# Relation sums of a graph network: rows of x3 W gathered from edges sorted on the chip, in place of dense count tables

## The reference

```python
def rgcn(x, src, dst, edge_type, weight, root, bias):
    out = x @ root + bias
    for r in range(8):
        mask = edge_type == r
        sums = segment_sum(x[src] * mask[:, None], dst, num_segments=1250)
        cnt = segment_sum(mask, dst, num_segments=1250)
        out = out + (sums / maximum(cnt, 1)[:, None]) @ weight[r]
    return out

u = rgcn(x3, ...)
z = concatenate([u, x3], axis=1) @ w_gate + b_gate
h = tanh(u) * z + x3 * (1 - z)
out = layernorm(x3 + h)
```

## Time and profile before

| what | us |
|---|---|
| runs of the kernel, median of 3 | 3798.32 |
| lowest and highest of them | 3790.24, 3836.48 |
| span of the profiled execution (first to last instruction) | 3698.9 |
| median less the profiled span | 99.4 |
| PE, DVE, ACT, Pool busy in that span | 3462.3, 2038.9, 939.7, 1363.0 |

### The profile page before, as it was taken

The page is one execution under the profiler, slowest core; times in us unless marked ns, Lnnn a source line. Parts: engine busy times, 40 slices in busy tenths (PEclk is TensorE's granted clock), DMA queues, the critical chain, the costliest instruction groups (busy, mean ns, idle before and its releaser), DMA issues.

```text
span 3698.9 us, 55829 instructions
## 1 busy us (share of the span) xinstructions
PE 3462.3 (94%) x22823; PEld 2642.5 (71%) x22823; DVE 2038.9 (55%) x4393; ACT 939.7 (25%) x1365; POOL 1363.0 (37%) x1094
## 2 busy tenths in 40 slices
PE   5898868999999999989989979899999999999998
PEld 4566556899899899934434478677777777777798
DVE  7877656432433454364443367777676544444477
ACT  0112313111211312222222266342222122222134
POOL 3767625566455567757777211300000000000021
PEclk8999989999999999989999989999999999999999
DMA  8789785543643455544554355543432422222233
GB/s 286 197 258 280 252 288 145 158 123 82 180 120 95 138 179 163 165 146 158 167 165 137 113 220 186 175 178 108 147 128 74 143 78 82 71 82 72 70 109 107
DMA packets 268704, 557.27 MB, mean 151 GB/s; under 512 B 94954, under 2 KB 118143, under 8 KB 266430
## 3 DMA queue, kind: packets, MB, share of 16 engines
q1 hardware_dynamic: 124504, 384.00, 29.6%
q10 hardware_dynamic: 64520, 116.89, 8.9%
q0 software_dynamic: 79424, 52.83, 8.8%
HBM read 370.13 MB, written 183.44 MB: 150 GB/s over the span
## 4 chain that ended last, share of the span: by engine, by line
PE 70%; DVE 11%; DMA 7%; POOL 6%; issue 4%; ACT 2%; SPq 1%; ACTq 0%; POOLq 0%; DVEq 0%
PE ps L442 50%; PE ps L825 11%; DMA EM<-ee,adr 2%; POOL EM L2483 2%; PE ps L447 2%; POOL gl L2493 2%; POOL gr L2493 2%; DVE eqj L989 2%; DVE eqj L986 2%; DMA slab<-T 1%; PE ps L710 1%; PE ps L712 1%; PE ps L711 1%; PE ps L491 1%; PE ps L492 1%
## 5 line engine op out<-in xcount | busy, mean ns | idle before, releaser
L442 PE MATMUL ps<-a,yy 128*128 128x384 f16 (+5 forms) x3200 | 429.2, 296 | 10.4 <-DVE yy L1685 9.0
L442 PE MATMUL ps<-wb,xh 128*128 128x256 f16 (+1 forms) x2560 | 427.7, 274 | 8.3 <-DVE xl L1257 5.4
L825 PE MATMUL ps<-mh,whl 128*128 128x384 f16 (+5 forms) x2048 | 426.3, 301 | 8.3 <-DVE ml L1832 7.5
L2444 POOL DMA_INDIRECT TR<-cnt,adr x167 | 277.2, 1660 | 362.0 <-DMA TR<-cnt,adr 345.7
L2533 POOL TENSOR_TENSOR graw<-graw,rsb 128x1280 f32<-128x1280 f32 (+1 forms) x2 | 5.7, 2854 | 1098.7 <-DMA graw<-GD 1098.7
L442 PEld LDWEIGHTS ps<-a,yy 128*128 128x128 f16 (+1 forms) x3200 | 311.6, 98 | 127.2 <-DVE yy L1685 9.3
L442 PE MATMUL ps<-wb,xl 128*128 128x256 f16 (+1 forms) x1280 | 350.2, 274 | 0.0
L710 PE MATMUL ps<-sl,x 128*128 128x512 f16 (+1 forms) x800 | 308.0, 385 | 29.8 <-ACT ue L2165 23.0
L2444 POOL DMA_INDIRECT T<-cnt,adr x167 | 271.9, 1628 | 133.6 <-DMA T<-cnt,adr 78.3
L711 PE MATMUL ps<-sl,x 128*128 128x512 f16 (+1 forms) x800 | 307.6, 384 | 0.0
L712 PE MATMUL ps<-sl,x 128*128 128x512 f16 (+1 forms) x800 | 307.4, 384 | 0.0
(11 more groups left out here) (355 smaller groups left out, 6913.1 us busy)
## 6 DMA issues: line engine op xcount, KB each, us to landing
TR<-zero_w SPq DMA_DIRECT2D x80, 625.0 KB, 4.7
EM<-neg ACTq DMA_DIRECT2D x40, 625.0 KB, 3.5
wraw<-in_L_gnn_weight SPq DMA_DIRECT2D x48, 512.0 KB, 3.3
UD<-ue ACTq DMA_DIRECT2D x90, 256.0 KB, 3.1
uu<-UD SPq DMA_DIRECT2D x45, 512.0 KB, 6.2
ar<-TR SPq DMA_DIRECT2D x72, 320.0 KB
eb<-EM SPq DMA_DIRECT2D x9, 2500.0 KB, 10.1
ar<-TR SPq DMA_DIRECT2D x72, 305.0 KB
```

What stands on the lines that cost most here:

```text
L442: i = pe.matmul(ap, l, r, start=(q == 0), stop=(q == len(pairs) - 1))
L825: ins = pe.matmul(ps[:, 0:cn], l, r, start=(q == 0), stop=(q == len(pairs) - 1))
L2444: return pool.indirect_dma_start(out=flat, out_offset=bass.IndirectOffsetOnAxis(ap=adr[:, n, t:t + 1], axis=0), in_=cnt[:, n, t:t + 1], in ...
```

## The change

- **Nothing of TR is left**: its 80 zero fills, DUP1's equal keys, the 167 adds, the reading as a16, `count`, `places` and the aggregation with it go. So does the early multiplication of x2 by root and w_gate (1304 to 1577 us).
- **NBR goes from 5 to 7**: seven relations are folded (112 slabs in place of 80) and seven have UD groups beside the edge loop (14 in place of 10, with NS = 16 slab buffers). SPLIT_SLAB has a new formula.
- **Edges are sorted on the chip by tiles of 128 destination nodes**, in SAGE's layer 0: DVE writes digits of the key dst*8+relation and one-hot rows of them (`one_hot_digits`, eight times 21 columns x (80 + 128)); PE counts by 167 products (`histogram`), so that 1/count per (dst, relation) is had (CI, written by SP); eight more products and some 35 DVE operations (`places_in_buckets`, `all_of_buckets`, `starts_of_buckets`, `slots`) give each edge its place in a list in which every tile starts at a multiple of 384. Pool issues 167 `times`, 167 gathers of 1/count and 167 scatters of records (row of y, node in the tile, 1/count, 0; 16 B) into REC, all ahead of the attention's gathers.
- **Rows of y for all edges' sources**: y = x3 W_r, 8 x 1250 rows of 4 KB, is stored in HBM (YD). For relations 0 to 6, 140 tiles of 128 x 512: PE `up_part` (6 products), DVE `add_up` (plus UD, loaded as 256 KB by SP), ACT `put_y` (scale, and the 256 KB store from ACT's queue). Relation 7, root and the x3 half of w_gate have no early part; they are multiplied from x3 (`late_part`, 240 products a group, two groups each). Relation 7's groups are g = 0 and 1, one after r = 2 and one after r = 6. The groups of root and gate, g = 2 to 5 in 96 units of 10 products on average, stand between the chunks below.
- **Gather and add.** The sorted list has NSLOT = 65 slots of three chunks of 128 edges, NCK = 195 chunks. For each chunk Pool gathers 128 rows of YD (4 KB each, six buffers gm; places not filled have an index out of bounds), ACT and DVE scale and split them (`high_rows`, `low_rows`), PE multiplies a 128 x 128 one-hot by both parts (`add_rows`, four products). After three chunks DVE takes the slot's sum, adding the slot before where it is of the same tile (`gather_sum`), and Pool scatters it to UA (`put_sum`, skipped but for a tile's last slot). Gathers start when all of YD is stored.
- **A new end, per tile of nodes**: UA, root's and gate's sums (RD) and x3 are loaded, u = UA + root part, its tanh (ACT), u turned and split, 48 gate products, Pool's tanh(u) - x3, DVE `finish`, normalisation and store.
- UA's zero fill is one DMA of 5 MB; x2 is kept as an f16 pair and the attention's W_down is split in f16.

The diff, cut to what is spoken of:

```diff
...
-NBR = 5
...
+NBR = 7
+NLATE = NREL - NBR
 YS = 56.0
 BH = 2 * NBR
-NW = 8 * (16 - BH) + 16
-UP_AT = {max(2 * r - 3, 0): r for r in range(1, NBR)}
-NS, NU = 11, 4
-SX2 = 248
+NS, NU, NS2 = 16, 6, 11
...
+NTILE = NT
+NCH = 3
+NSLOT = (ET * EP + NTILE * (128 * NCH - 1)) // (128 * NCH)
+NCK = NSLOT * NCH
+SKIP = 16384.0
+REC_PAD = 128 * NCK
...
+LATE_G = 2 * NLATE
+ALL_G = LATE_G + 4
+PASSES = [[(0, 1, 2, 3, 4), (5, 6, 7, 8, 9)]] * LATE_G + [[(0, 1, 2, 3), (4, 5, 6), (7, 8, 9)]] * 4
...
+HELD = 8
+UNITS = [(g, n, k) for g in range(LATE_G, ALL_G) for n in range(3) for k in range(8)]
+AHEAD = 3
+BETWEEN = [range(AHEAD + (len(UNITS) - AHEAD - HELD) * c // NCK, AHEAD + (len(UNITS) - AHEAD - HELD) * (c + 1) // NCK)
+           for c in range(NCK)]
+LAG2 = 2
...
-SPLIT2 = [behind(17.3 * (n - 2) - 10) for n in range(16)]
-SPLIT_WA = [behind(17.3 * (n + 1) - 10) for n in range(16)]
-SPLIT_SLAB = [behind((215, 215, 232, 232, 250, 250, 250, 250, 267, 267, 267)[q] if q < NS else
...
+SPLIT_SLAB = [behind(53.0 * (q // 8 - 1) + 6.6 * (q % 8)) if q >= NS else 0 for q in range(8 * BH)]
...
-            more = iter(DUP1)
...
-                for ts, _ in [g for _, g in zip(range(3), more)]:
-                    equal_keys(1, ts, 5 if n < 12 else 4)
...
+            def histogram(m):
+                if m == 0:
+                    psum.take("hist", b=7)
+                    w.wait_ge(*psum.empty("hist"))
+                w.wait_ge(*V("hob", m))
+                for j, t in enumerate(HP[m]):
+                    i = pe.matmul(psum.at("hist")[0:80, 0:128], hoa[m % 2][:, j, :], hob[m % 2][:, j, :], start=(t == 0),
+                                  stop=(t == ET - 1))
+                i.then_inc(*P.tick("hist", m))
...
+                        if (layer, q) == (0, 1) and i >= 2:
+                            histogram(i - 2)
+                        if (layer, q, i) == (0, 3, 5):
+                            places_in_buckets()
...
-            for n in range(16):
...
-            for n, (h, rel) in enumerate(HALVES[0:BH]):
...
+            def up_part(r, i, j):
+                t, c = vv[(2 * r + j) % 2], slice(128 * i, 128 * i + ROWS[i])
+                ps = psum.take("y3", r, i, j)
+                w.wait_ge(*V("v", r, j))
+                w.wait_ge(*V("gs"))
+                w.wait_ge(*psum.empty("y3", r, i, j))
+                sum_of(ps[0:ROWS[i], :], [p for k in range(2) for p in (
+                    (gsh[:, k, c], t[:, 0, k, :]), (gsh[:, k, c], t[:, 1, k, :]), (gsl[:, k, c], t[:, 0, k, :]))]).then_inc(
...
+            for r in range(NBR):
+                for j in range(2):
+                    for i in range(NT):
+                        up_part(r, i, j)
+                        if (r, j, i) == (0, 0, 5):
+                            spread_scales()
+                        if r == 1 and j == 0:
+                            turn_x3(i)
+                if r == 2:
+                    for n in range(2):
+                        for k in range(8):
+                            late_part(0, n, k)
+            for g in range(1, LATE_G):
+                for n in range(2):
+                    for k in range(8):
+                        late_part(g, n, k)
...
+            def add_rows(c):
+                s, cc = c // NCH, c % NCH
+                w.wait_ge(*V("rows", c))
+                w.wait_ge(*V("ml", c))
+                for j in range(2):
+                    if cc == 0:
+                        psum.take("slot", s, j, b=4 + 2 * (s % 2) + j)
+                        w.wait_ge(*psum.empty("slot", s, j))
+                    for q in range(2):
+                        ins = pe.matmul(psum.at("slot", s, j)[:, :], one_hots(c), ms[c % NMS][:, q, 512 * j:512 * j + 512],
+                                        start=(cc == 0 and q == 0), stop=(cc == NCH - 1 and q == 1))
...
+            for c in range(NCK):
+                add_rows(c)
+                for n in BETWEEN[c]:
+                    late_part(*UNITS[n], bank=0)
...
+            def one_hot_digits(m):
+                t0, n = HP[m][0], len(HP[m])
+                if m >= 2:
+                    w.wait_ge(*P("hist", m - 2))
+                w.wait_ge(*V.now())
+                for to, x, width in ((hoa, ca, 80), (hob, cb, 128)):
+                    dve.tensor_tensor(to[m % 2][:, 0:n, :], x[:, t0:t0 + n, None].broadcast_to([EP, n, width]),
+                                      io[:, None, 0:width].broadcast_to([EP, n, width]), ALU.is_equal).then_inc(
+                        *V.tick("hob", m))
...
+            def add_up(r, i, j):
+                n, rk = (2 * r + j) * NT + i, ROWS[i]
+                t = yb[n % 20]
+                w.wait_ge(*P("y3", r, i, j))
+                w.wait_ge(*u_in[n // 4 % 5](n // 4))
+                o = psum.taken_out(V, "y3", r, i, j)
+                V.at["y", n] = V.n
+                dve.tensor_tensor(t[0:rk, :], psum.at("y3", r, i, j)[0:rk, :], t[0:rk, :], ALU.add).then_inc(*o)
...
+            def low_rows(c):
+                w.wait_ge(*A("mh", c))
+                dve.scalar_tensor_tensor(out=ms[c % NMS][:, 1, :], in0=gm[c % NGB][:, :], scalar=rc[:, c, 2:3],
+                                         in1=ms[c % NMS][:, 0, :], op0=ALU.mult, op1=ALU.subtract).then_inc(*V.tick("ml", c))
...
+            def gather_sum(s):
+                a = rr[s % NRR]
+                if s >= NRR:
+                    w.wait_ge(*r_put[s % NRR](s - NRR))
+                w.wait_ge(*V.now())
+                for j in range(2):
+                    o = slice(512 * j, 512 * j + 512)
+                    w.wait_ge(*P("slot", s, j))
+                    t = psum.taken_out(V, "slot", s, j)
+                    V.at["rr", s] = V.n
+                    if s == 0:
+                        dve.tensor_copy(a[:, o], psum.at("slot", s, j)[:, :]).then_inc(*t)
+                    else:
+                        dve.scalar_tensor_tensor(out=a[:, o], in0=rr[(s - 1) % NRR][:, o], scalar=mt[:, 0, s:s + 1],
...
+            for c in range(NCK + LAG2):
+                if c < NCK:
+                    low_rows(c)
+                if c == LAG2:
+                    for n in range(AHEAD):
+                        after_unit(n)
+                if c >= LAG2:
+                    if (c - LAG2) % NCH == NCH - 1:
+                        gather_sum((c - LAG2) // NCH)
...
+            def whole_sum(i):
+                r, a = ROWS[i], i % 2
+                w.wait_ge(*sum_in[a](i))
+                dve.scalar_tensor_tensor(out=ua[a][0:r, :], in0=ua[a][0:r, :], scalar=cm[0:r, NREL:NREL + 1], in1=ro[a][0:r, :],
+                                         op0=ALU.mult, op1=ALU.add).then_inc(*V.tick("u", i))
+                w.wait_ge(*V.now())
+                dve.tensor_reduce(out=um[0:r, i:i + 1], in_=ua[a][0:r, :], axis=AX.X, op=ALU.max,
+                                  apply_absolute_value=True).then_inc(*V.tick())
...
+            def finish(i):
+                r, a = ROWS[i], i % 2
+                w.wait_ge(*zx_in[a](i))
+                for j in range(2):
+                    o = slice(512 * j, 512 * j + 512)
+                    w.wait_ge(*P("gate", i, j))
+                    dve.scalar_tensor_tensor(out=zq[a][0:r, o], in0=psum.at("gate", i, j)[0:r, :], scalar=ud[0:r, i:i + 1],
+                                             in1=zq[a][0:r, o], op0=ALU.mult, op1=ALU.add).then_inc(*psum.taken_out(V, "gate", i, j))
                     w.wait_ge(*V.now())
...
+                    if j == 0:
+                        w.wait_ge(*G("th", i))
+                        if i >= 3:
+                            w.wait_ge(*out_put[i % 3](i - 3))
+                    dve.tensor_tensor(zq[a][0:r, o], zq[a][0:r, o], th[a][0:r, o], ALU.mult).then_inc(*V.tick("z", i))
                     w.wait_ge(*V.now())
...
+                    dve.scalar_tensor_tensor(out=oo[i % 3][0:r, o], in0=xr[a][0:r, o], scalar=2.0, in1=zq[a][0:r, o], op0=ALU.mult,
+                                             op1=ALU.add).then_inc(*V.tick("o", i))
                     w.wait_ge(*V.now())
...
+                    dve.bn_stats(stb[0:r, i, j, :], oo[i % 3][0:r, o]).then_inc(*V.tick())
+                aggregate(i, 2)
+                rstd(dve, w, "rs4", i, i + 1)
...
+            def put_y(r, i, j):
+                n, rk = (2 * r + j) * NT + i, ROWS[i]
+                t = yb[n % 20]
+                w.wait_ge(*V("y", n))
+                w.wait_ge(*V("rsx"))
+                act.mul(t[0:rk, :], t[0:rk, :], rsx[0:rk, i:i + 1]).then_inc(*A.tick("y", n))
+                w.wait_ge(*A("y", n))
+                act.dma_start(YD[N * r + 128 * i:N * r + 128 * i + rk, 512 * j:512 * j + 512], t[0:rk, :]).then_inc(
+                    *y_out[n // 4 % 5].tick(n // 4))
...
+            def high_rows(c):
+                w.wait_ge(*g_in[c % NGB](c))
+                for s in y_out:
+                    w.wait_ge(*s("last"))
+                if c >= NMS:
+                    w.wait_ge(*P("ck", c - NMS))
```

(45 more changed lines are left out.)

1793 lines of the change are left out of this document (821 added, 972 removed).

## The result

The changed kernel took 4077.26 us (median of 4, 4060.36 to 4085.7) where the kernel before took 3807.39 beside it: a ratio of 1.0695 [1.064, 1.0749], 7% slower. The forecast was 3382 us and faster, so it was wrong in sign, and its range (3290 to 3530) was missed by more than 500 us.

What follows compares the result with a forecast made beforehand. TensorE (PE) bound the kernel, busy 94% of the span, with Pool's queue nearly as long in the edge loop. Stage ends of 2659 and 3093 us plus a 190 us tail gave span 3283, plus 99 made 3382 us; range 3290 to 3530.

Steps and rivals of the forecast that it cites:

- Pool's queue now holds 501 issues there: SAGE stage: 501 small DMA issues at 1.33 us, 667 us from about 593 to 1260, 80 us ahead of the edge loop.
- rival 3: Gather stage: Pool's queue delivers one large gather at a time, 916 to 1150 us, total 3864 to 4098 us; chance 0.10.
- The fixed 99.4 us: Whole kernel: the median's excess over the profiled span of 3698.9 us, taken as fixed and added at the end.
- First 1300 us: Before the edge loop: +6 us up to 623 us and +25 in SAGE, so Pool's chain starts at 1309 + 31 = 1340.
- Edge loop: Pool's chain of three issues a column, 4.46 us each, lasts 745 us, until 2085, and sets the end after PE.
- y stage: Making rows y = x3 W_r with relation 7's groups: 356 us at 320 GB/s, gathering starts at 2659.
- Rival 2: y and gather stages: transfers bound at 250 GB/s, y 412 us, gathering 456, total 3460 us; chance 0.21.
- Gather stage: 195 chunks: DVE the longest at 391 us, with a 10% loss for waiting 434 us, ending at 3093.
- the 0.90: Gather stage: DVE busy at 90%, from a chosen 10% loss to waits that takes its 391 us to 434.
- Rival 1: y and gather stages: no losses, gathering at DVE's 391 us and y at PE's 313, total 3296 us; chance 0.17.
- Rival 4: Gather stage's empty places are moved too (+47 us) and edge loop keeps 767 us (+22): 3440 to 3450; chance 0.04.
- Tail: After gathering: 190 us in all, DVE's ten tiles at 14.3 us making 143, with 10 us for Pool's subtraction.

Runs made afterwards that it cites:

- the control: The changed kernel unedited, run again on a chip without slowing: 3369.95 us against 3700.77 for the kernel before, a ratio of 0.9098.
- after_pair: The changed kernel unedited, on slowing chip 9: 4079.28 us against 3817.16 for the kernel before, a ratio of 1.069.
- probe_halfud: Changed kernel with respaced small DMAs in the streams and one of three products left out of the groups beside the edge loop: 3519.57 us, kernel before 3696.32.
- no_low_rows: Changed kernel with already-met waits in its streams, gathered rows' low halves and two of four products a chunk left out: 3325.03 us, kernel before 3711.6.
- drain8: Changed kernel, every eighth small DMA of each stream waiting until those ahead landed: 3444.47 us (0.9297 of the kernel before); on slowing chip 9 3764.41 (0.986).
- oldwait: Changed kernel with an already-met wait ahead of each small DMA in all three streams: 3376.32 us, timed again 3371.85 (0.911 of the kernel before).

## Why the prediction was wrong, and where it was right

By its own steps, with the control's numbers (span 3369.1), which stand for the work alone:

- **The step that failed** is in the SAGE part: "Pool's queue now holds 501 issues there", 667 us "to 1260: ahead of the edge loop by 80 us". I priced the streams as Pool's own time, with PE beside them untouched; the bounds +13 to +60 held only DVE's and PE's new work. On a slowing chip each stream all but stops PE and what feeds on it: after_pair's edge loop starts at 1949 us, the control's at 1312. That is 637 of the 709 us between the two times; the edge loop has 34 more and the stretch up to z's last sum 30. The prediction named the right sign, "if PE has idle time in SAGE beyond 25 us", but put no price on it. No rival had it: rival 3, my only slower case, put a Pool queue on the path later, at the 4 KB gathers, and those ran as forecast. Nothing in the earlier trace rows shows 1.25 us for more than a few DMAs in a row: in the edge loop, 1.49 us on average and with a wait at each third. I had used that very number as evidence against rival 3 and never asked what a denser stream would do. What the runs put in its place: on a slowing chip PE is busy for 10 to 13% while such a stream runs, on the others the step holds (the third stream ends at 1274, 38 us ahead of the edge loop). What makes a chip slow stays open.
- **The fixed 99.4 us** was the same thing unrecognised. The profiled span of 3698.9 and the median of 3798.32 must come from chips of both kinds, since each has the value of one; for one execution span and time differ by 1.8 us (3369.1 and 3370.87). Without it the forecast for a chip without slowing is 3285 and not 3382; that 3382 is near the measured 3370 is luck, 85 us of missing terms set off by 97 that don't exist.
- **First 1300 us**: +31 forecast, 2 measured (gather of XL at 1311.8, before at 1309.4), by two terms that cancel. SAGE's products take 26 us more, where the sum had +25; they start 23 us earlier, where it had +6 with a lower bound of −10. SAGE's first group of products, with its first and last start, in the kernel before and in the control:

```profile
L442 PE MATMUL ps<-wb,xh x2560: 270/273/421, 623.5 to 1241.0; 128*128 128x256 f16 x178, 128*98 128x256 f16 x19
L446 PE MATMUL ps<-wb,xh x2560: 270/273/421, 600.7 to 1243.9; 128*128 128x256 f16 x178, 128*98 128x256 f16 x19
```

  So the first 623 us were priced too dear. From 24 to 452 us the DMA share fell from 0.84 to 0.68 and DVE's work from 343 to 300 us, while PE's rose from 368 to 385; which of the two freed PE no run separates.
- **Edge loop**: right in kind and size. 745 forecast for Pool's chain, 772 measured; 1340 to 2085 forecast, 1312 to 2083 measured. Taking 273 us of PE away brought next to nothing there, and probe_halfud shows why: PE's work is not what holds it.
- **y stage**: 356 forecast, 418 measured, the largest miss of size. Rival 2's 412 has the number, but its cause only in part: 27 MB less gave 21 us, the factor's handover 52. The handover was in no sum: VD's next piece is loaded only after PE's last product with the old one, ACT splits it behind ten stores in its programme, DVE's half follows.
- **Gather stage**: 434 forecast, 428 measured, DVE the bound (380 of 428 us busy, 89%), as forecast; the 0.90 held, though the reason given for it, that DVE ran "at no more than 70%" in full stages before, misreads (343 of 428 us, 80%, in the first stretch). The loop of six buffers decided little: Pool waited for DVE's split 24 times, 19 us in all. A gather of 512 KB landed after 6.0 us; the prediction had taken about 5, and the figure quoted under rival 3 was 3.2.
- **Rivals 1, 3 and 4**: Rival 1's y at 313 us and gathering at 391 didn't come. Rival 3's gathers one at a time (4.7 us a chunk) didn't either: 195 in 428 us are 2.2 us each. Rival 4's empty places were skipped: the indirect DMAs moved 137 MB, and the rows of YD, XL, XR and UA alone make 136.

```profile
q0 software_dynamic: 98896, 137.13, 15.2%
```

- **Tail**: 190 forecast, 219 measured. Loads with two buffers, in no term of the sum, are 22 of the 29. Pool's subtraction cost 13 us where I had taken 10, and the lines rose as the row of 2180 ns said. This case's runs show the rule of the Trainium skill ("SBUF — State Buffer", Who interferes with whom) on the same instruction with and without the GpSimd one beside it: 1254 and 692 ns.
- The Trainium skill ("DMA: Bandwidth & Descriptors", Specifications) states about 358 GB/s of HBM for a core, by which y and gathering would run at their engines' pace. No run here tests that figure: the two stages moved 236 and 258 GB/s, no_low_rows' gathering 299, and y was held mostly by its handover.

## What to carry to other kernels

Look at what a change adds to a queue not only for its length but for its density: a stream denser than any in the trace has no price in it, and one of its rivals is that the engines beside it slow down. Time the unedited kernel beside every experiment, on the same chip: two runs here (drain8 and oldwait) seemed to prove a remedy on a chip where there was nothing to remedy, and the met waits did nothing on a slowing one either. When a median and a profiled span differ by far more than launch costs, find out why before adding the difference.

## What the hardware showed that I had not expected

On chips 6, 9 and 14, and on the one of the record, an unbroken stream of small indirect DMAs (128 pieces of 4 to 16 B each, 1.25 to 1.28 us apart) all but stops PE: a product each 2.80 us, with 1.40 us between a weight load and the product behind it; busy for 10 to 13% in the three streams of the record. The granted clock fell to 0.50, the level of 1.2 GHz, which matters little beside that (a product took 0.37 us in place of 0.27). With an even 1.49 us and nothing waited for PE was at 96%, at 2.2 us at 100%. On chips without slowing the unedited kernel had PE busy for 175 of 180 us in the first stream, and for all of 60 us at 1.25 us apart. The gathers of 4 KB rows, 2.2 us apart, took 429 to 437 us on slowing chips and 423 to 433 on the others.

Whether VectorE and ScalarE are slowed themselves or only wait for PE's sums, no run separates. The first hole of the record hints at how PE is held up:

```profile
675.84 2.40 PE L451 MATMUL ps<-ident,bp 128*128 128x128 f32 x10 [27.19 <-DVE am L1213]
681.82 1.11 PE L451 MATMUL ps<-ident,bp 128*128 128x128 f32 x4 [3.59 <-issue]
692.47 0.69 PE L451 MATMUL ps<-ident,bp 128*128 128x128 f32 x2 [9.54 <-issue]
```

After standing for 27 us PE ran ten products with their weight loads at once, and then ran dry. Twenty instructions in 27 us are 1.4 us each, the pace of the second hole. So it looks as if instructions reach the engine slowly and gather ahead of it while it waits. VectorE's seven instructions in a row from 675.02 us stand behind 10.3 us of "issue", again some 1.4 us each. That is a reading of one stretch, not an experiment. The DMAs that load the program are not what got slow: in the second hole there were 4, the longest 1.4 us, in the control's second stream 19, up to 1.8 us. Which part of the chip gives way, and what makes chips differ, the runs leave open.
